# Two-layer mixture kernel: samples issued ahead of two broadcasts, three weight splits moved to GpSimd, and a new order of the last steps

## The chip, the cores and the metric

One core of one Trainium2 chip runs the whole program. The metric is the time of one execution on the device in microseconds (us). TensorE (PE) multiplies matrices, VectorE (DVE), ScalarE (ACT) and GpSimd (POOL) do elementwise work, and each has its own instruction stream. SyncE (SP) issues nearly all DMAs. The engines meet only at semaphores.

## The reference

128 sequences of 64 tokens and 256 features go through two conditional layers, in float32:

```
h = gelu(x @ Wi[e] + bi[e]);  r = h @ Wo[e] + bo[e] + x      # e: one of 8 experts of the sequence
y = normalize(r, 1e-12) * gamma[e] + beta[e]
a = gelu(y @ down_W.T + down_b)                              # 256 -> 64
o = a @ expert_W[d].T + expert_b[d], or a where d is invalid # d: one of 16 domains of the sequence
u = (o + emb[d]) @ up_W.T + up_b + y
out = normalize(u, 1e-5) * ln_gamma + ln_beta
```

## The kernel before, in words

**Tiles.** The sequences are sorted by expert on the chip. A tile is two sequences (128 tokens), and there are 64 tiles. The last four are mixed: their two sequences can have different experts, so most of their instructions exist once per half.

**Precision.** Every float32 operand of a large product is held as a high and a low half in float16, and a product takes three matmuls (high by high, high by low, low by high). For a weight chunk of 128x512, `high` on ScalarE writes the rounded part and `low` on VectorE writes what is left. An expert has 8 chunks: four of Wi and four of Wo.

**Steps.** The function `step(i, ...)` exists once per engine. In step i TensorE runs the first product of tile i (`p_h`, lines 1168 to 1170), the `up` product of tile i-4 (`p_u`, 1207 and 1208), the `down` product of tile i-3 (`p_d`, 1192 to 1194), the second product of tile i-1 (`p_o`, 1179 to 1181) and the transposition of tile i-2 (`p_t`, 1215). Steps 0 to 3 also build the table `ctab` of up_W folded with the experts of layer two, in four rounds (line 1108 on TensorE, 684 on ScalarE, 912 on VectorE). Steps 64 to 68 are the drain: no first product is left, and they run out the tiles in flight.

**What sets the order.** Each engine executes the program as written, and each wait sits in its own place of that order. SP issues in one queue, in program order: at the start the first expert's chunks, the next expert's first four chunks (`stage`), then the broadcast of `bo` and of `gamma` over 128 partitions (1 MB each), then the loads of step 0: `load_turned(2)` (x of tile 2, transposed, line 404) and `load_natural(0)` (line 411). The first product of a tile needs `x_hi` and `x_lo` (lines 698 and 899), which need `x_T`.

**GpSimd.** In step i it adds `bo` to the natural x of tile i-1 (line 630), computes two reciprocal square roots (614 for the first normalization, 635 for the second), multiplies by gamma (609, or 602 and 605 for a mixed tile) and copies the per-expert columns: `gb_tile` (643, for the multiplication of `yT_hi` on ScalarE, line 777) and `bi_tile` (575). Each copy or gamma product of a mixed tile first loads two expert numbers into registers. In step 1 it also runs `split_rows` (lines 554 to 562), which splits the shared rows of the table in three parts. SP sends them out to memory in `added` and back into `ctab`.

Of the kernel before, what the change touches and what calls it, by code (L numbers as in the profile page):

```python
# [4 lines left out]
B, S, D = 128, 64, 256  # L5
# [50 lines left out]
def build(nc, t):  # L56
# [4 lines left out]
    with ctx:  # L61
# [173 lines left out]
        w_first_hi = sem("w_first_hi")  # L235
        w_first = sem("w_first")
# [128 lines left out]

        def late(j):

            return isinstance(j, int) and TILES - 4 <= j < TILES
# [13 lines left out]
        FIRST_ORDER = (0, 2, 1, 3, 4, 5, 6, 7)  # L382

        @block.sync
        def _(sp):
# [61 lines left out]
            def step(i, parity, four, weights):  # L447
# [26 lines left out]
                if exists(i):  # L474
                    load_natural(b[0:2], i, parity)
                if weights and starting:
                    load_chunk()
                if isinstance(i, int) and i == 1:
# [3 lines left out]
                if isinstance(i, int) and i == 2:  # L482
# [3 lines left out]
                    for q in range(PARTS):  # L486
                        sp.dma_start(ctab[A + PARTS + E0 * q:A + PARTS + E0 * (q + 1), :, 1, :],
                                     by_part[q, ENTRIES:ENTRIES + E0, :].unsqueeze(1)
                                     .to_broadcast([E0, ENTRIES, D])).then_inc(added_in, 16)

# [6 lines left out]
        def _(pool):  # L497
# [82 lines left out]
            def step(i, parity, four, weights):  # L580
                e_third, e_before, e_last, _, e_next = indices(pool, i + (IDX_EXP - 3), 5, E0 - 1)
                if exists(i - 5) and not late(i - 5):
# [53 lines left out]
                if exists(i - 2):  # L636

                    need(pool, a1o_done, i - 3)
                    if isinstance(i, int) and i == 2:
                        pool.wait_ge(g_scaled, 1)  # L640
                        pool.wait_ge(downb_ready, 1)
                    for n, e_n in enumerate(experts(i - 2, e_before)):
                        ins = pool.tensor_copy(gb_tile[:, parity, n, :], gb_flat[:, bass.ds(e_n * GB, GB)])
                    ins.then_inc(gb_done, 1)
# [11 lines left out]
        def _(act):  # L656
# [43 lines left out]

            for n, m in enumerate(FIRST_ORDER):

                if n == 2:
                    high_x(0, 0)
                if n == 4:
                    act.wait_ge(beta_down, 1)
                    act.wait_ge(adapter_in, 6 * 16)
                    nc.scalar.activation(gb_c[:, :, KD:KD + 1], ph_flat[1][:, WCH:WCH + E0].unsqueeze(2), ACT.Identity,
# [636 lines left out]
```

## Time and profile before

| | us |
|---|---|
| median of 3 runs | 470.23 (469.9 to 473.76) |
| the profiled execution | 468.74 |
| its span in the profile | 467.0 |
| TensorE busy | 435.8 (93%) |
| VectorE, ScalarE, GpSimd busy | 392.2, 378.4, 343.1 |

The span is what the profile's rows cover, and the profiled execution is 1.74 us longer than it. Times of rows count from the start of the span. A row that says "idle before" gives how long its engine had nothing to run and which operation ended that. The ends of matmul rows are modelled: matmuls overlap, and a row of 0.22 us can stand 0.06 us after the one before it, so the pace is read from the starts.

### The profile page before, as it was taken

The numbers are of one execution on the slowest core, as the hardware profiler recorded it, in microseconds if no ns is written. First come the engines' busy times: TensorE is split into PE (matmuls) and PEld (weight loads), VectorE is DVE, ScalarE is ACT, GpSimd is POOL, SyncE is SP. The second block draws the span as 40 slices with busy tenths as digits, with TensorE's granted clock in tenths as the row PEclk, the third lists the DMA queues.
The fourth block names the chain that finished last, engine by engine and source line by source line (L and its number), as shares of the span: only waits on it lengthen the run. The fifth ranks groups of instructions, "written<-read, shape, count | busy, mean of one in ns | idle before, by whom it ended". The sixth has DMA issues, their size and how long they took to land.

```text
span 467.0 us, 19001 instructions
## 1 busy us (share of the span) xinstructions
PE 435.8 (93%) x5724; PEld 399.7 (86%) x5725; DVE 392.2 (84%) x1049; ACT 378.4 (81%) x1161; POOL 343.1 (73%) x560
## 2 busy tenths in 40 slices
PE   2977999999999999999999999999999999999962
PEld 2765989998999989998999899998999999888951
DVE  7748999998899989998899989998899887776574
ACT  2767988888988888988888988888988877877722
POOL 3035488888788877888788878887788888866652
PEclk9999999999999999999999999999999999999995
DMA  4964234433333333433333333333332222220101
GB/s 105 314 220 94 77 85 132 113 107 108 110 96 97 104 104 107 109 96 98 101 105 104 111 95 96 107 106 107 106 91 78 63 69 63 66 59 27 30 19 34
DMA packets 51178, 45.71 MB, mean 98 GB/s; under 512 B 8820, under 2 KB 42563, under 8 KB 50883
## 3 DMA queue, kind: packets, MB, share of 16 engines
q1 hardware_dynamic: 50385, 45.02, 34.3%
q8 instruction: 20, 0.33, 0.3%
q10 hardware_dynamic: 754, 0.20, 0.2%
q14 instruction: 19, 0.16, 0.1%
HBM read 36.75 MB, written 8.44 MB: 97 GB/s over the span
## 4 chain that ended last, share of the span: by engine, by line
PE 84%; DVE 3%; issue 3%; ACT 3%; SPq 2%; DMA 2%; POOL 2%; POOLq 1%; ACTq 0%; DVEq 0%
PE p_h L1168 12%; PE p_o L1179 12%; PE p_o L1180 12%; PE p_o L1181 12%; PE p_h L1170 11%; PE p_h L1169 11%; PE p_u L1207 3%; PE p_u L1208 3%; PE p_t L1215 3%; DMA x_nat<-in_x 2%; PE p_d L1192 2%; PE p_d L1194 1%; PE p_d L1193 1%; ACT h L729 1%; ACT yT_hi L777 1%
## 5 line engine op out<-in xcount | busy, mean ns | idle before, releaser
L1168 PE MATMUL p_h<-x_hi,W 128*128 128x128 f16 (+1 forms) x1088 | 185.2, 218 | 4.2 <-DVE x_lo L899 2.3
L1170 PE MATMUL p_h<-x_hi,W 128*128 128x128 f16 (+1 forms) x1088 | 184.9, 217 | 0.0
L1169 PE MATMUL p_h<-x_lo,W 128*128 128x128 f16 (+1 forms) x1088 | 184.9, 217 | 0.0
L729 ACT ACTIVATE h<-p_h,bi_tile 128x128 f32<-128x128 f32 (+1 forms) x544 | 149.5, 360 | 0.1
L1179 PE MATMUL p_o<-W,h_hi 128*128 x512 | 139.6, 273 | 0.4 <-DVE r L947 0.4
L1180 PE MATMUL p_o<-W,h_hi 128*128 x512 | 139.6, 273 | 0.0
L1181 PE MATMUL p_o<-W,h_lo 128*128 x512 | 139.6, 273 | 0.0
L1168 PEld LDWEIGHTS p_h<-x_hi,W 128*128 x1088 | 105.8, 98 | 13.2 <-issue 5.5
L1169 PEld LDWEIGHTS p_h<-x_lo,W 128*128 x1088 | 106.1, 99 | 0.8
L1170 PEld LDWEIGHTS p_h<-x_hi,W 128*128 x1088 | 106.0, 98 | 0.0
L933 DVE SCALAR_TENSOR_TENSOR h_lo<-h,h_hi 128x512 f16<-128x512 f32 (+1 forms) x128 | 97.9, 767 | 1.9 <-ACT h_hi L740 1.9
L590 POOL TENSOR_TENSOR y<-y,lng 128x256 f32<-128x256 f32 x60 | 43.7, 728 | 54.6 <-DVE h_lo L933 52.4
L740 ACT ACTIVATE h_hi<-h 128x512 f16<-128x512 f32 (+1 forms) x128 | 80.1, 629 | 2.0
L635 POOL TENSOR_TENSOR rs<-mv,neg_half 128x1 f32<-128x1 f32 x64 | 58.9, 920 | 13.4 <-DVE mv L979 13.1
L754 ACT ACTIVATE a<-p_d,gb_tile 128x128 f32<-128x128 f32 (+1 forms) x68 | 24.1, 360 | 53.8 <-PE p_d L1194 53.8
L630 POOL TENSOR_TENSOR x_nat<-x_nat,bo_t 128x256 f32<-128x256 f32 x60 | 46.6, 776 | 15.3 <-DMA x_nat<-in_x 15.3
L1179 PEld LDWEIGHTS p_o<-W,h_hi 128*128 128x128 f16 x512 | 50.1, 98 | 6.0 <-issue 1.2
L1181 PEld LDWEIGHTS p_o<-W,h_lo 128*128 128x128 f16 x512 | 50.1, 98 | 5.8
L1180 PEld LDWEIGHTS p_o<-W,h_hi 128*128 128x128 f16 x512 | 50.1, 98 | 5.1
L974 DVE SCALAR_TENSOR_TENSOR a1s<-a,a1s 64x128 f16<-64x128 f32 x64 | 22.1, 346 | 34.6 <-ACT a1s L759 34.4
L614 POOL TENSOR_TENSOR rs<-mv,neg_half 128x1 f32<-128x1 f32 x64 | 35.2, 550 | 18.0 <-DVE mv L962 16.1
L777 ACT ACTIVATE yT_hi<-p_t,gb_tile 128x128 f16<-128x128 f32 (+1 forms) x136 | 42.2, 380 | 7.5 <-PE p_t L1215 5.6
(170 smaller groups left out, 935.1 us busy)
## 6 DMA issues: line engine op xcount, KB each, us to landing
stage<-in_w SPq DMA_DIRECT2D x56, 256.0 KB, 2.7
x_nat<-in_x SPq DMA_DIRECT2D x128, 64.0 KB, 2.1
out<-y SPq DMA_DIRECT2D x128, 64.0 KB, 2.0
x_T<-in_xT SPq DMA_DIRECT2D x126, 64.0 KB, 2.0
W<-in_w SPq DMA_DIRECT2D x8, 256.0 KB, 3.8
bo_t<-in_bo SPq DMA_DIRECT2D x1, 1024.0 KB, 7.1
g_t<-in_gamma SPq DMA_DIRECT2D x1, 1024.0 KB, 10.2
W<-in_expert_W SPq DMA_DIRECT2D x2, 128.0 KB, 2.8
```

The lines of the kernel that those rows point to most:

```text
L630: pool.tensor_tensor(x_nat[:, 1 - parity, :], x_nat[:, 1 - parity, :], bo_t[:, bass.ds(e_last * D, D)], ALU.add).then_inc(xb_done, 1)
L635: pool.tensor_tensor(rs[:, 1:2], mv[:, 1, 1:2], neg_half[:, 0:1], ALU.pow).then_inc(rs2_done, 1)
L729: ins = nc.scalar.activation(h[:, c, mine], p_h[parity][:, c, mine], ACT.Gelu, bias=bi_tile[:, parity, n, c:c + 1], scale=1.0 / (XS * WS))
L740: ins = nc.scalar.activation(out, h[:, cols_h, mine], ACT.Copy, scale=HS)
L777: ins = nc.scalar.activation(yT_hi[:, k, mine], turned_z[:, mine], ACT.Copy, scale=gb_tile[:, parity, n, k:k + 1])
L933: ins = v.scalar_tensor_tensor(lo[at], h[:, cols_h, mine], HS, hi[at], ALU.mult, ALU.subtract)
L1168: mm(out, hi, x_high, start=(k == 0), stop=False)
L1169: mm(out, hi, x_low, start=False, stop=False)
L1170: ins = mm(out, lo, x_high, start=False, stop=(k == KD - 1))
L1179: mm(p_o[:, 0:D], h_high[at], hi, start=(j == 0 and n == 0), stop=False)
L1180: mm(p_o[:, 0:D], h_high[at], lo, start=False, stop=False)
L1181: ins = mm(p_o[:, 0:D], h_low[at], hi, start=False, stop=(j == KI - 1 and n == len(places) - 1))
```

## The change

- **SP:** of the next expert's four chunks only the first is issued early. Then come x_T of tile 2 and natural x of tile 0, then `bo`, then the other three chunks, then `gamma`. Step 0 issues neither of the two again. The round trip of `added` moves from steps 1 and 2 to steps 2 and 3, and goes ahead of the chunk load of its step.
- **GpSimd:** the high parts of the first expert's chunks 5, 6 and 7 are made here instead of on ScalarE, and `split_rows` moves from step 1 to step 0.
- **ScalarE and VectorE:** x of tile 1 is split before chunk 4, and the plain entries of `ctab` (lines 717 and 923) move from ahead of step 0 to its end.
- **Drain:** GpSimd copies `gb_tile` at the start of the step. TensorE runs `down` ahead of `up`. ScalarE waits for its own `a1o` before it writes `a1`, and issues the DMA of the second half of the last tile, which SP issued before.

```diff
@@ sync
-            for j in range(AHEAD):
+            load_later(0, expert[0], 0, 0)
+            b = indices(sp, IDX_SP, 4, B - 1)
+            load_turned(b[2:4], 2, 0)
+            load_natural(b[0:2], 0, 0)
+            sp.dma_start(bo_t[:, :], t["bo"].partition_broadcast(P)).then_inc(bo_in, 16)
+            for j in range(1, AHEAD):
                 load_later(j, expert[0], j, j % SLOTS_W)
-            sp.dma_start(bo_t[:, :], t["bo"].partition_broadcast(P)).then_inc(bo_in, 16)
...
-                if exists(i + 2):
+                if exists(i + 2) and not first:
                     load_turned(b[2:4], i + 2, parity)
...
-                    for n in range(2):
+                    for n in range(1 if last_tile(i - 5) else 2):
...
-                if isinstance(i, int) and i == 1:
+                if isinstance(i, int) and i == 2:
 
                     sp.wait_ge(parts_ready, 1)
@@ gpsimd
+                if exists(i - 2) and drain(i):
+                    gather_gb()
                 if exists(i - 5) and not late(i - 5):
...
+                if exists(i - 2) and not drain(i):
+                    gather_gb()
                 if exists(i + 1):
                     gather_bi(e_next, i + 1, 1 - parity)
-                if isinstance(i, int) and i == 1:
+                if isinstance(i, int) and i == 0:
+                    for m in FIRST_ORDER[ACT_FIRST:]:
+                        pool.wait_ge(first_in[m], 16)
+                        pool.tensor_scalar(W[m][:, 0:1, :, 0, :], by_unit(first_stage[m]), WS, None, ALU.mult)\
+                            .then_inc(w_pool_hi, 1)
                     pool.wait_ge(u_ready, 1)
@@ scalar
+                    if drain(i):
+                        act.wait_ge(a1o_done, i - 3)
...
+            b = indices(act, 6 * (STEPS - 1) + IDX_SP + 5, 1, B - 1)
+            act.wait_ge(y_late, TILES - (TILES - 4))
+            act.dma_start(t["out"][bass.ds(b[0] * S, S), :], y[HALF[1], (TILES - 1) % 2, :])\
+               .then_inc(y_out[(TILES - 1) % 2], 16)
@@ vector
+                if n < ACT_FIRST:
+                    dve.wait_ge(w_first_hi, n + 1)
+                else:
+                    dve.wait_ge(w_pool_hi, n + 1 - ACT_FIRST)
@@ tensor
+                    if drain(i):
+                        pe.wait_ge(a1_done, i - 3)
...
+                    if drain(i) and c == UP_AT and exists(i - 3):
+                        down()
                     if c == UP_AT and exists(i - 4):
...
-                    if c == DOWN_AT and exists(i - 3):
+                    if c == DOWN_AT and exists(i - 3) and not drain(i):
                         down()
```

**SP, from the end of the first expert's chunks to step 0.** `x_T` is the transposed x (here of tile 2), `x_nat` the natural x (here of tile 0). Before:

```order
L418 DMA stage<-in_w 128x512
...
L438 DMA bo_t<-in_bo 128x2048
L439 DMA g_t<-in_gamma 128x2048
...
L297 TENSOR_LOAD idx [waits idx_ready]
L404 ISA [waits x_split]
L404 DMA x_T<-in_xT 128x128
...
L411 DMA x_nat<-in_x 64x256
```

The same place in the change:

```order
L428 DMA stage<-in_w 128x512
L298 TENSOR_LOAD idx
L414 ISA [waits x_split]
L414 DMA x_T<-in_xT 128x128
...
L421 DMA x_nat<-in_x 64x256
...
L451 DMA bo_t<-in_bo 128x2048
...
L454 DMA g_t<-in_gamma 128x2048
```

Both sample loads now stand ahead of the two broadcasts, and three of the four chunks stand between the broadcasts.

**GpSimd, step 65 of the drain.** `gb_tile` holds the columns of tile 63, `yg` is the gamma product of tile 62, the first `rs` is the first normalization of tile 63. Before:

```order
L297 TENSOR_LOAD idx [waits yl_done,z1_done]
L602 ISA
L602 TENSOR_TENSOR yg<-z,g_t 64x256
L605 ISA [waits yg_half]
L605 TENSOR_TENSOR yg<-z,g_t 64x256
L614 TENSOR_TENSOR rs<-mv,neg_half 128x1 [waits mv1_done,yg_done]
L635 TENSOR_TENSOR rs<-mv,neg_half 128x1 [waits mv2_done]
L297 TENSOR_LOAD idx [waits a1o_done]
L643 ISA
L643 COPY gb_tile<-gb_c 128x4
```

In the change:

```order
L298 TENSOR_LOAD idx [waits a1o_done]
L605 ISA
L605 COPY gb_tile<-gb_c 128x4
...
L298 TENSOR_LOAD idx [waits yl_done,z1_done]
L630 ISA
L630 TENSOR_TENSOR yg<-z,g_t 64x256
L633 ISA [waits yg_half]
L633 TENSOR_TENSOR yg<-z,g_t 64x256
L642 TENSOR_TENSOR rs<-mv,neg_half 128x1 [waits mv1_done,yg_done]
L663 TENSOR_TENSOR rs<-mv,neg_half 128x1 [waits mv2_done]
```

The wait for `a1o_done` moved from behind the gamma products and both `rs` to the front of them.

**TensorE, step 66 of the drain.** `p_u` is `up` of tile 62, `p_d` is `down` of tile 63. Before:

```order
L1207 MATMUL p_u<-ctab,a1s 128x256 [waits a1o_done,a1_lo,r2_done]
L1208 MATMUL p_u<-ctab,a1o 128x256
...
L1192 MATMUL p_d<-yT_hi,down_hi 128x128 [waits yT_done]
L1193 MATMUL p_d<-yT_lo,down_hi 128x128
L1194 MATMUL p_d<-yT_hi,down_lo 128x128
```

In the change:

```order
L1234 MATMUL p_d<-yT_hi,down_hi 128x128 [waits a1_done,yT_done]
L1235 MATMUL p_d<-yT_lo,down_hi 128x128
L1236 MATMUL p_d<-yT_hi,down_lo 128x128
...
L1300 ISA x2
L1249 MATMUL p_u<-ctab,a1s 128x256 [waits a1o_done,a1_lo,r2_done]
L1250 MATMUL p_u<-ctab,a1o 128x256
```

The two products changed places, in steps 64, 65 and 66.

## Rows read from the trace of the kernel before

**Rows 1.** Busy time by stretch: stretch, its length, then PE, PEld, DVE, ACT, POOL.

```profile
50.00:434.00 384.00, 381.06 (x5144) 354.43 (x5142) 336.57 (x896) 334.02 (x1029) 311.48 (x480) 1.00 0.34 94
```

**Rows 2.** TensorE's waits from 15 to 45 us: in total, times, longest.

```profile
PE p_h L1168 <- DVE x_lo L899: 2.3, 2, 1.3
PE p_t L1215 <- DVE z L986: 1.8, 1, 1.8
PE p_u L1108 <- DVE ctab L912: 1.7, 1, 1.7
PE p_d L1192 <- DVE yT_lo L1016: 1.0, 1, 1.0
```

**Rows 3.** Timeline of ScalarE: start, length, operation, idle before.

```profile
29.99 0.42 ACT L698 ACTIVATE x_hi<-x_T 128x256 f16<-128x256 f32 x1 [4.58 <-DMA x_T<-in_xT]
```

**Rows 4.** Timeline of GpSimd, steps 1 and 2.

```profile
30.56 0.88 POOL L630 TENSOR_TENSOR x_nat<-x_nat,bo_t 128x256 f32<-128x256 f32 x1 [15.34 <-DMA x_nat<-in_x]
...
31.99 0.39 POOL L558 CAST W<-W 128x256 f16<-128x256 f32 x1
...
32.91 1.00 POOL L562 TENSOR_TENSOR W<-W 128x256 f32<-128x256 f32 x1
...
36.22 0.39 POOL L560 COPY W<-W 32x256 f16<-32x256 f16 x1
```

**Rows 5.** DMA issues from 0 to 45 us: count, KB each, median us to landing.

```profile
bo_t<-in_bo SPq DMA_DIRECT2D x1, 1024.0 KB, 7.1
g_t<-in_gamma SPq DMA_DIRECT2D x1, 1024.0 KB, 10.2
```

**Rows 6.** Timeline of SP's queue: start and length of issuing.

```profile
15.76 1.94 SPq L418 DMA_DIRECT2D stage<-in_w  x4
...
17.74 0.42 SPq L438 DMA_DIRECT2D bo_t<-in_bo  x1
...
20.96 0.88 SPq L404 DMA_DIRECT2D x_T<-in_xT  x2
...
41.33 0.34 SPq L485 DMA_DIRECT2D ctab<-added  x1
```

**Rows 7.** The tile ctab from 36 to 60 us: its first reader in `up`.

```profile
L1207 PE MATMUL p_u<-ctab,a1s x4: 269/272/273, 50.3 to 56.8; 128*128 x4
```

**Rows 8.** Timeline of GpSimd in the drain.

```profile
449.47 0.72 POOL L602 TENSOR_TENSOR yg<-z,g_t 64x256 f32<-64x256 f32 x1 [0.26 <-issue]
...
453.33 0.55 POOL L614 TENSOR_TENSOR rs<-mv,neg_half 128x1 f32<-128x1 f32 x1 [2.23 <-DVE mv L962]
...
454.90 0.38 POOL L643 COPY gb_tile<-gb_c 128x4 f32 x2
...
456.68 0.72 POOL L605 TENSOR_TENSOR yg<-z,g_t 64x256 f32<-64x256 f32 x1 [0.19 <-POOL yg L602]
```

**Rows 9.** Timeline of ScalarE in the drain.

```profile
451.14 0.78 ACT L785 ACTIVATE a1o<-a,gb_tile,keeps 128x64 f16<-128x64 f32 x2
...
455.38 0.93 ACT L777 ACTIVATE yT_hi<-p_t,gb_tile 128x64 f16<-128x64 f32 x4 [1.47 <-POOL gb_tile L643]
```

**Rows 10.** Timeline of TensorE in the drain, steps 65 to 67.

```profile
454.58 0.44 PE L1215 MATMUL p_t<-ident,z 128*128 128x128 f32 x2 [1.57 <-DVE z L986]
457.10 0.37 PE L1207 MATMUL p_u<-ctab,a1s 128*128 x1 [2.08 <-ACT a1o L785]
...
457.90 0.31 PE L1192 MATMUL p_d<-yT_hi,down_hi 128*128 128x128 f16 x1
...
460.45 0.37 PE L1207 MATMUL p_u<-ctab,a1s 128*128 x1 [1.70 <-ACT a1o L785]
```

**Rows 11.** Timeline of VectorE in the drain, step 66.

```profile
458.14 0.43 DVE L957 SCALAR_TENSOR_TENSOR yg<-p_u,yg 128x256 f32<-128x256 f32 x1 [0.95 <-PE p_u L1208]
...
459.81 0.29 DVE L974 SCALAR_TENSOR_TENSOR a1s<-a,a1s 64x128 f16<-64x128 f32 x1
```

**Rows 12.** Timeline of SP's queue at the end: the last tile's two halves.

```profile
463.93 1.14 SPq L472 DMA_DIRECT2D out<-y  x2
```

More of the change, by code:

```diff
@@ L235, in build @@
         w_first_hi = sem("w_first_hi")
+        w_pool_hi = sem("w_pool_hi")
         w_first = sem("w_first")
@@ L364, in drain, with last_tile @@
             return isinstance(i, int) and i >= TILES
+        def last_tile(j):
+            return isinstance(j, int) and j == TILES - 1
         def late(j):
@@ L382, in build, with by_unit @@
         FIRST_ORDER = (0, 2, 1, 3, 4, 5, 6, 7)
+        ACT_FIRST = 5
+        def by_unit(staged):
+            return staged.rearrange("p (a u q) -> p a u q", a=1, u=2)
         @block.sync
@@ L463, in step @@
                     b = record[6 * parity:6 * parity + 6]
-                if exists(i + 2):
+                first = isinstance(i, int) and i == 0
+                if exists(i + 2) and not first:
                     load_turned(b[2:4], i + 2, parity)
@@ L489, in step @@
                                      .to_broadcast([E0, ENTRIES, D])).then_inc(added_in, 16)
+                if weights and starting:
+                    load_chunk()
             run(sp, step, NCH, AHEAD, 2 * LEAD)
@@ L581, in step, with gather_gb @@
                 e_third, e_before, e_last, _, e_next = indices(pool, i + (IDX_EXP - 3), 5, E0 - 1)
+                def gather_gb():
+                    need(pool, a1o_done, i - 3)
+                    if isinstance(i, int) and i == 2:
+                        pool.wait_ge(g_scaled, 1)
+                        pool.wait_ge(downb_ready, 1)
+                    for n, e_n in enumerate(experts(i - 2, e_before)):
+                        ins = pool.tensor_copy(gb_tile[:, parity, n, :], gb_flat[:, bass.ds(e_n * GB, GB)])
+                    ins.then_inc(gb_done, 1)
+                if exists(i - 2) and drain(i):
+                    gather_gb()
                 if exists(i - 5) and not late(i - 5):
@@ L699, in high_x @@
                     .then_inc(xhi_done, 1)
[L701 removed]
+            for n, m in enumerate(FIRST_ORDER[:4]):
                 if n == 2:
                     high_x(0, 0)
[L705 to L708, printed above, removed]
[L709 to L711 removed]
                 act.wait_ge(first_in[m], 16)
                 high(m, 0, first_stage[m]).then_inc(w_first_hi, 1)
[L716 to L718 removed]
+            act.wait_ge(beta_down, 1)
+            act.wait_ge(adapter_in, 6 * 16)
+            nc.scalar.activation(gb_c[:, :, KD:KD + 1], ph_flat[1][:, WCH:WCH + E0].unsqueeze(2), ACT.Identity,
+                                 bias=downb[:, :]).then_inc(downb_ready, 1)
+            act.wait_ge(u_summed, 1)
+            nc.scalar.copy(u_s[:, :], ph_flat[1][:, 0:D]).then_inc(u_ready, 1)
+            high_x(1, 1)
+            for m in FIRST_ORDER[4:ACT_FIRST]:
+                act.wait_ge(first_in[m], 16)
+                high(m, 0, first_stage[m]).then_inc(w_first_hi, 1)
             def gelu(i, parity, half):
@@ L743, in step @@
             def step(i, parity, four, weights):
-                if exists(i + 1):
+                if exists(i + 1) and not (isinstance(i, int) and i == 0):
                     high_x(i + 1, 1 - parity)
@@ L791, in step @@
                     high_h(i, parity, 1)
+                if isinstance(i, int) and i == 0:
+                    act.wait_ge(up_in, 2 * 16)
+                    nc.scalar.activation(ctab[:, E1:ENTRIES, 0, :], upT[:, :].unsqueeze(1).to_broadcast([P, 2, D]),
+                                         ACT.Copy, scale=CS).then_inc(c_plain_hi, 1)
                 if isinstance(i, int) and i == 1:
@@ L1057, in step @@
                     normal_1()
-                if exists(i + 1):
+                if exists(i + 1) and not (isinstance(i, int) and i == 0):
                     low_x(i + 1, 1 - parity)
@@ L1072, in step @@
                     low_y()
+                if isinstance(i, int) and i == 0:
+                    dve.wait_ge(c_plain_hi, 1)
+                    v.scalar_tensor_tensor(ctab[HALF[0], E1:ENTRIES, 1, :], rows(upT[HALF[0], :], 2), CS,
+                                           ctab[HALF[0], E1:ENTRIES, 0, :], ALU.mult, ALU.subtract).then_inc(c_plain, 1)
                 if isinstance(i, int) and i == 1:
```

26 lines of the change are left out of this document (4 added, 22 removed).

## The prediction

> **What bounds the kernel now.** I read the busy time by stretch first. From 50 to 434 us TensorE is busy 381.06 of 384.00 us [rows 1]: the middle is its own, the change does not touch it, and what is won or lost at either end passes through unchanged. So I read the waits of TensorE at the start, then the timelines of the engines it waits for, and last the drain from 449 us.
>
> At the start TensorE waits four times where the change acts: 1.3 us for `x_lo` of tile 2, 1.7 for `ctab` of round 1, 1.8 for `z` of tile 0, 1.0 for `yT_lo` of tile 0 [rows 2]. (The other wait in the 2.3 of the first row is before the first matmul.) They have one source. `x_T` of tile 2 is issued at 20.96 [rows 6], behind 2 MB of broadcasts that land at 17.74 + 7.1 = 24.8 (`bo`) and 10.2 after their issue (`gamma`) [rows 5]. ScalarE stands still for 4.58 us until 29.99 [rows 3], and its `ctab` copies, its `h` and its `yT_hi` are late with it. GpSimd stands still for 15.34 us until natural x of tile 0 is there at 30.56. Then it runs `split_rows` from 31.99 to 36.22 + 0.39 = 36.61 [rows 4], ahead of the `rs` that `z` of tile 0 needs.
>
> In the drain the chain runs from one engine to the next and every wait is short, so each place in an engine's order counts.
>
> **The start.** SP issues a chunk in 1.94 / 4 = 0.49 us [rows 6]. Without three chunks ahead of them the sample loads go out near 17.2 (0.9 us of it for their addresses) instead of 20.96, with only the chunks still queued in front. A landing near 21 is my estimate; ScalarE needs it at 29.99 - 4.58 = 25.4, and the 0.5 us for the plain table entries that now stand ahead of that place are taken from an earlier one. So `x_hi` of tile 2 comes 4.6 us earlier. TensorE ends the second product of tile 0 no earlier than before, so of those 4.6 us the first wait gives only its 1.3; the `ctab` copies of round 1 come earlier by the same 4.6, so the 1.7 goes too. On GpSimd `split_rows` (4.6 us) runs from about 21 to 26 beside work that doesn't need it, `bo` lands near 24 (it has 0.75 MB of chunks less and 0.25 MB of samples more in front), so `rs` of tile 0 waits for VectorE alone and the 1.8 goes. The 1.0 on `yT_lo` goes if ScalarE holds its lead. Sum: 1.3 + 1.7 + 1.8 + 1.0 = 5.8 us.
>
> What could be late next: ScalarE and VectorE then run without a break until step 3, and by adding up their operations `yT_lo` of tile 0 comes about 0.4 us before TensorE wants it. Chunk 1 of the next expert now stands behind `bo` and must be there at 25.4 + 0.4 = 25.8. The order of the queue says about 25. And the `ctab` writes from `added` move back one step. Before, they went out at 41.33 [rows 6] and were wanted at 50.3 [rows 7]; after, they wait behind natural x of tile 3, so I put their issue near 38.8 and the want at 44.5, 5.7 us later against 9.0. I take 0.1 us for these three together and 0 to 1 as the range. **Start: 5.7 us won.**
>
> **The three high parts on GpSimd.** No row has this operation. The nearest cheap one is a cast of 128x256 in 0.39 us, so 0.8 for 512 columns; the dear end is the two-input subtraction of 128x256 at 1.00, so 2.0 [rows 4]. I take 1.0, nearer to the cast, since it has one input too. VectorE's low parts of these chunks stand ahead of its round-0 entries of `ctab`, which TensorE wants at about 25.8. From 17.9, when chunk 5 should be there by its issue, three at 1.0 end at 20.9 and VectorE is through at about 25.1. From 1.5 us each TensorE waits, 3 us for every further microsecond: 1.5 us at the dear end. Cost taken: 0. The work that falls away on ScalarE is worth nothing by itself, since it stood still for 4.58 us right after [rows 3].
>
> The Trainium skill, "GPSIMD Engine Reference", sections 1 and 4.1, says that one-input work on GpSimd is roughly at line rate, two-input work about twice as slow, and that it shares its memory interface with VectorE instructions that have two inputs there, which the low parts are. By that the operations of the two engines could follow each other instead of overlapping and the sum would lose some tenths more at the start; no row before has this pair, so the bounds above stand.
>
> **The drain, columns first.** In step 65 GpSimd used to multiply tile 62 by gamma at 449.47, in the shade of TensorE's last long product, and was free when `rs` of tile 63 came due at 453.33 [rows 8]. Now the copy of `gb_tile` stands in front, and it waits for `a1o` of tile 61, which ends at 451.14 + 0.78 = 451.92 [rows 9]. After that: 0.7 for the wake-up and the load of two expert numbers (copy starts at 452.6), then from that copy to the end of the second gamma product as before, 456.68 + 0.72 - 454.90 = 2.5 (until 455.1), then `rs` at 455.2 instead of 453.33: 1.87 later. Before, `rs` ended at 453.88 and the transposes at 454.58 + 0.44 = 455.02 [rows 10], 1.14 later; now 455.75 + 1.14 = 456.9. `yT_hi` of tile 63 waited at 455.38 for its columns [rows 9]. The columns are now early, and it starts at about 456.95: 1.5 later. The same move in step 64 pushes GpSimd by about 1.4, which ends before 450.
>
> **The drain, down first.** In step 66 `up` of tile 62 started at 457.10 and `down` of tile 63 at 457.90 [rows 10]. `down` was ready at about 457.2 by `yT_lo`. With the 1.5 it is ready at 458.8, runs 0.65 at the slow pace (four matmuls of `up` took 0.8 there, half clock, 1.2 GHz), and `up` follows at about 459.4, so VectorE's `yg` of tile 62 starts at 460.3 instead of 458.14. On VectorE the low part of `a1s` of tile 63 stands 459.81 - 458.14 = 1.67 behind it [rows 11], so it ends at 460.3 + 1.67 + 0.29 = 462.3, and the last `up` starts at 462.5 instead of 460.45 [rows 10]: **2.05 lost.** Even with `yT_hi` in time, down first alone would push that `up` by about 0.5, because `a1s` on VectorE hangs behind `yg`. The wait for `a1o` on ScalarE is for its own work of the step before: 0.
>
> **The last half by ScalarE.** SP issues two halves in 1.14 us, 0.57 each plus the address [rows 12]. The second leaves beside the first: **0.65 won**, 0.5 to 0.7.
>
> **Sum.** -5.7 + 2.05 - 0.65 = -4.3 us. Against the profiled execution, 468.74 - 4.3 = 464.4 (span 462.7). That execution is 1.5 us under the median of the runs, and I make the forecast against the median: 470.23 - 4.3 = **465.9 us**. 1% is 4.7 us, about what a measurement of this kernel can tell from no change, so the bound for faster is 465.5.
>
> **The rivals.**
> - *The sum holds*: 465.9, chance 0.45. Its own spread is 0.7 us, so four in ten of it lie under 465.5.
> - *The drain costs nothing*: GpSimd or TensorE is not on the path as I read it, the move hides, and only the 0.65 is left: 470.23 - 5.8 - 0.65 = 463.8. For it speaks that `yT_hi` did wait for its columns for up to 1.47 us [rows 9], which is what the move attacks; against it that the columns were only 0.26 us behind the transposes (455.28 against 455.02). Chance 0.22.
> - *The start gives less*: GpSimd at 2.0 us each (1.5 lost) or the ports, chunk 1 or the table writes late by as much: 467.5. For it speak the slacks of 0.4 us and less; chance 0.24.
> - *Slower*: chunk 1 of the next expert lands with the end of the queue. ScalarE then stops at the chunk as it did at the sample, and each microsecond after 25.8 costs TensorE one. `gamma`, issued right behind `bo` at about 18.2, landed at 18.2 + 10.2 = 28.4 [rows 5, 6], and `x_T` of tile 2, the last thing ScalarE waited for, at 29.99 [rows 3]; the loads behind it ended at about 31. At 31.1 the start keeps 5.7 - 5.3 = 0.4, and the drain's 1.4 outweighs it: 471.2. It turns to slower from a landing at 30.1. Against it: the chunk is issued ahead of `gamma`, and `bo` did land at 24.8, long before `gamma`. Chance 0.06.
> - *It does nothing at the start*, because the sample loads wait for something else: the load for tile 2 also waits for `x_lo` of tile 0. Against it: SP gets there only after the first chunk, issued at 15.76 [rows 6], when that is done. 470.2 + 1.4 = 471.6, chance 0.03.
>
> The Trainium skill, "TensorE: Matmul & The Clock Gate", part 1, says that an idle array falls to half clock. The last steps agree: four matmuls of 256 columns take 457.90 - 457.10 = 0.8 us [rows 10], the pace of 1.2 GHz, after a pause of 2.08. A longer pause before the transposes of step 65 could add 0.2 us of half clock to the drain; the sum does without it.
>
> **Chances and range.** Faster by over 1%: 0.45 x 0.4 + 0.22 = 0.40, and 0.02 of the third case, 0.42. Slower by over 1% (over 474.9): 0.04, for what I have not seen. Within 1%: 0.54. The range takes the second case with its 6.2 + 0.65 (463.3), the third, and the unknown costs' ends: 463.0 to 468.8.
>
> **What would show it.** Right: `x_hi` of tile 2 near 25.2 with no idle on ScalarE, TensorE without the four waits, `rs` of tile 63 about 1.9 later against the end of the last long product, the last `up` 2 later, one output issue per queue at the end. Wrong: high parts on GpSimd over 1.5 us, ScalarE idle before its chunk 1, an idle TensorE before the first `up`, or a last `up` that isn't later.

## The result: 1.7 to 2.3 us faster, where 4.3 were forecast

| | before | changed |
|---|---|---|
| median of 20 runs each | 470.69 (469.16 to 473.76) | 468.98 (466.83 to 471.16) |
| ratio | | 0.9951, 95% interval 0.9935 to 0.9967 |
| profiled execution, its span | 468.74, 467.0 | 469.78, 468.0 |

The change saves 1.7 us by the medians and 0.49%, or 2.3 us, by the ratio; its interval lies wholly under 1. The forecast was 465.9, with a range up to 468.8; the median lies 0.2 above that range. The profiled execution of the changed kernel is 0.8 above its median, that of before 2.0 below, so the two spans must not be subtracted. I cut each execution at three marks instead, the transposes of tile 4, 60 and 62 (starts in us):

| execution | tile 4 | 60 | 62 | end | 4 to 60 | 62 to end |
|---|---|---|---|---|---|---|
| before | 67.98 | 431.40 | 449.92 | 467.0 | 363.4 | 17.1 |
| before, once more | 67.55 | 430.92 | 449.45 | 466.5 | 363.4 | 17.1 |
| changed | 64.63 | 430.52 | 448.96 | 468.0 | 365.9 | 19.1 |
| changed, once more | 64.60 | 429.04 | 447.39 | 466.5 | 364.4 | 19.1 |

The start won 2.9 to 3.4 us (forecast 5.7). Three kernels of the experiments leave the start as it is in the changed kernel (e1, e4 and e11); their marks of tile 4 are 63.96, 63.76 and 65.01, so the start itself varies by 1.25 us between executions, and differences of some tenths at this mark say little. The drain with the output lost 2.0 (forecast 2.05 - 0.65 = 1.4). The stretch between, which no edit touches, differs by up to 2.5 us between executions; the last section shows what goes with it.

**The start in the changed kernel.** TensorE's waits from 15 to 50 us (in total, times, longest) answer to [rows 2]:

```profile
PE p_t L1148 <- DVE ctab L947: 2.7, 1, 2.7
PE p_h L1208 <- DVE x_lo L934: 1.0, 1, 1.0
PE p_d L1234 <- DVE yT_lo L1052: 1.0, 1, 1.0
```

The waits for `x_lo` of tile 2 and for `z` are gone. What is left of `x_lo` is the wait ahead of the first matmul. The wait for `yT_lo` is as long as before, and there is one of 2.7, for the table entries of round 0. It is 1.3 in the second execution. It is not wholly new, though: [rows 2] come from one execution of before, and the other has in place of the 1.3 for `x_lo` of tile 2 a wait of 1.3 for the same entries:

```profile
PE p_t L1108 <- DVE ctab L912: 1.3, 1, 1.3
```

Timeline of ScalarE (start, length, operation, idle before), to be read beside [rows 3]:

```profile
21.28 0.63 ACT L683 ACTIVATE W<-stage 128x512 f16<-128x512 f32 x1 [2.81 <-DMA stage<-in_w]
...
26.51 0.44 ACT L723 ACTIVATE x_hi<-x_T 128x256 f16<-128x256 f32 x1
...
32.78 0.42 ACT L723 ACTIVATE x_hi<-x_T 128x256 f16<-128x256 f32 x1 [0.78 <-DMA x_T<-in_xT]
```

`x_hi` of tile 2 starts at 26.51 without a pause, 3.5 us earlier than the 29.99 of before. The sample of tile 3 is now the late one. The pause of 2.81 is one that the forecast did not have: ScalarE waits for chunk 0 of the next expert, issued at 15.84 and landed at 21.26. GpSimd and VectorE, beside [rows 4]:

```profile
19.00 4.47 POOL L671 TENSOR_SCALAR W<-W 128x512 f16<-128x512 f32 x3 [3.71 <-DMA W<-in_w]
...
27.03 2.14 POOL L578 TENSOR_TENSOR W<-W 128x256 f32<-128x256 f32 x1
```

```profile
18.50 0.69 DVE L938 SCALAR_TENSOR_TENSOR W<-W 128x512 f16<-128x512 f32 x1
20.58 1.10 DVE L938 SCALAR_TENSOR_TENSOR W<-W 128x512 f16<-128x512 f32 x1 [1.39 <-POOL W L671]
22.04 1.09 DVE L938 SCALAR_TENSOR_TENSOR W<-W 128x512 f16<-128x512 f32 x1 [0.36 <-POOL W L671]
23.50 0.86 DVE L938 SCALAR_TENSOR_TENSOR W<-W 128x512 f16<-128x512 f32 x1 [0.36 <-POOL W L671]
...
26.16 0.67 DVE L947 SCALAR_TENSOR_TENSOR ctab<-p_t,ctab 64x512 f16<-64x512 f32 x1
```

A high part on GpSimd takes 4.47 / 3 = 1.49 us, and VectorE waits for each one. The low part beside it takes 1.10 where the one before took 0.69, and a subtraction of `split_rows` takes 2.14 where it took 0.67 to 1.00 before. The first high part starts at 19.00, when its chunk is there (18.40 in the second execution), and not at 17.9 as forecast. So the low part of round 0's entries starts at 26.16, and TensorE goes on at 27.48 (27.35 in the second execution), where in the two executions of before it went on at 25.77 and 26.66.

**The drain in the changed kernel,** GpSimd, TensorE and VectorE, answering to [rows 8, 10, 11]. The transposes of tile 62 are at 448.96 here and were at 449.92, so 0.96 has to be added for a comparison:

```profile
451.86 0.31 POOL L605 COPY gb_tile<-gb_c 128x4 f32 x2 [2.29 <-ACT a1o L809]
...
454.43 0.55 POOL L642 TENSOR_TENSOR rs<-mv,neg_half 128x1 f32<-128x1 f32 x1
```

```profile
455.48 0.69 PE L1257 MATMUL p_t<-ident,z 128*128 128x128 f32 x2 [3.26 <-DVE z L1022]
458.09 0.29 PE L1234 MATMUL p_d<-yT_hi,down_hi 128*128 128x128 f16 x1 [1.92 <-DVE yT_lo L1052]
...
461.86 0.37 PE L1249 MATMUL p_u<-ctab,a1s 128*128 x1 [2.10 <-DVE a1s L1010]
```

```profile
459.80 0.42 DVE L993 SCALAR_TENSOR_TENSOR yg<-p_u,yg 128x256 f32<-128x256 f32 x1 [1.77 <-PE p_u L1250]
...
461.47 0.29 DVE L1010 SCALAR_TENSOR_TENSOR a1s<-a,a1s 64x128 f16<-64x128 f32 x1
```

`rs` of tile 63 comes 454.43 + 0.96 - 453.33 = 2.06 later (forecast 1.87) and the last `up` 461.86 + 0.96 - 460.45 = 2.37 later (forecast 2.05). The output leaves in one issue by ScalarE beside SP's:

```profile
465.35 0.57 ACTq L829 DMA_DIRECT2D out<-y  x1
```

### The profile page after: what moved, and what is told of

The parts are those of the page before. It is cut to its first block, busy times and chain, and to the rows that moved or that the text cites. A ratio compares the mean times of both kernels' runs of the same rounds, so it can differ in the third digit from the quotient of the medians.

```text
span 468.0 us, 19008 instructions
## 1 busy us (share of the span) xinstructions
PE 436.9 (93%) x5724; PEld 397.8 (85%) x5725; DVE 396.1 (85%) x1049; ACT 378.8 (81%) x1158; POOL 359.5 (77%) x563
## 4 chain that ended last, share of the span: by engine, by line
PE 84%; POOL 3%; DVE 3%; ACT 3%; issue 3%; DMA 2%; POOLq 1%; SPq 0%; DVEq 0%; ACTq 0%
PE p_h L1208 12%; PE p_o L1219 12%; PE p_o L1220 12%; PE p_o L1221 12%; PE p_h L1210 11%; PE p_h L1209 11%; PE p_u L1249 4%; PE p_t L1257 3%; PE p_u L1250 3%; PE p_d L1234 2%; PE p_d L1236 2%; PE p_d L1235 1%; ACT h L751 1%; DMA W<-in_w 1%; POOL W L671 1%
## 5 line engine op out<-in xcount | busy, mean ns | idle before, releaser
L969 DVE SCALAR_TENSOR_TENSOR h_lo<-h,h_hi 128x512 f16<-128x512 f32 (+1 forms) x128 | 95.9, 752 | 0.5 <-ACT h_hi L762 0.4
L663 POOL TENSOR_TENSOR rs<-mv,neg_half 128x1 f32<-128x1 f32 x64 | 58.0, 907 | 17.2 <-DVE mv L1015 16.9
L1010 DVE SCALAR_TENSOR_TENSOR a1s<-a,a1s 64x128 f16<-64x128 f32 x64 | 26.4, 413 | 35.3 <-ACT a1s L783 35.0
L591 POOL COPY bi_tile<-bi_c 128x8 f32 x68 | 45.8, 677 | 8.4 <-DVE idx L930 8.0
L620 POOL TENSOR_TENSOR y<-y,lnb 128x256 f32<-128x256 f32 x60 | 43.7, 729 | 4.7
```

Source lines behind the costliest of these rows:

```text
L591: ins = pool.tensor_copy(bi_tile[:, parity, n, :], bi_c[:, bass.ds(e_n * KI, KI)])
L663: pool.tensor_tensor(rs[:, 1:2], mv[:, 1, 1:2], neg_half[:, 0:1], ALU.pow).then_inc(rs2_done, 1)
L969: ins = v.scalar_tensor_tensor(lo[at], h[:, cols_h, mine], HS, hi[at], ALU.mult, ALU.subtract)
```

## The experiments

Theory: the order of SP's queue alone wins at the start. The high parts on GpSimd, and what they do to the operations of VectorE beside them, cost again what the other moves could have given, and the drain's two moves cost by their places in the order. Main rival: the drain cost less than it seemed, and the loss lay in the middle. Below, "under before" is the difference of the medians of runs on the same chip; e5 to e8 ran on one chip and the other experiments on a second, where the changed kernel has no runs. The mark "tile 4" is that of the table above.

### e1_old_drain: the drain of before

The edits of e11 and e4, whose diffs stand under the next heading, in one.

> The changed kernel with the drain of before: columns of gb_tile behind rs again, up ahead of down; the last half still by ScalarE, the start untouched. Theory (the drain moves cost time; from the last transposes of a pure step at 449.12 to the end the changed kernel took 18.9 us against 16.9, and 0.4 of output won is hidden in it): 2.4 us come back, 468.98 - 2.4 = 466.6, rs of tile 63 again about 4.3 us after those transposes and not 5.3. Rival (the drain's chain is set elsewhere and only this one execution showed it long): under 0.7 us, 468.3 or more.

Measured: 464.64 against 469.61, ratio 0.9887 (0.9868 to 0.9905), 5.0 under before. From tile 62 to the end it takes 16.7 us. Its `rs` of tile 63:

```profile
449.86 0.55 POOL L640 TENSOR_TENSOR rs<-mv,neg_half 128x1 f32<-128x1 f32 x1 [2.23 <-DVE mv L994]
```

That is 3.42 after the transposes of tile 62 (446.44), as before (3.41), and not 5.47. The 4.3 that I had written was a slip: it took the changed kernel's mark for both kernels. The drain's moves cost 19.06 - 16.69 = 2.4 us, and the rival falls. The last half by ScalarE is what is left against before: 17.06 - 16.69 = 0.37 us won, and not 0.65.

### e4_up_first and e11_columns_last: the two moves apart

e4 takes back TensorE's order and the two waits that came with it:

```diff
-                    if drain(i):
-                        act.wait_ge(a1o_done, i - 3)
-                    if drain(i):
-                        pe.wait_ge(a1_done, i - 3)
-                    if drain(i) and c == UP_AT and exists(i - 3):
-                        down()
-                    if c == DOWN_AT and exists(i - 3) and not drain(i):
+                    if c == DOWN_AT and exists(i - 3):
```

and e11 only GpSimd's:

```diff
-                if exists(i - 2) and drain(i):
-                    gather_gb()
-                if exists(i - 2) and not drain(i):
+                if exists(i - 2):
```

> The changed kernel with only TensorE's order of the drain back (up ahead of down, with the two waits that came with it gone); the columns of gb_tile stay first on GpSimd. By the working of the forecast 1.4 of the drain's cost comes from GpSimd and 0.65 from the order of TensorE: 468.98 - 0.65 = 468.3, rs of tile 63 as late as in the changed kernel, last up 0.6 earlier. Rival (the order is the whole cost): 466.6, as with the whole drain of before.

> The changed kernel with only GpSimd's order of the drain back (rs ahead of the columns of gb_tile); TensorE keeps down ahead of up. The other half of the drain's two moves: from the transposes of tile 62 to the end it took 19.04 with both, 18.46 with columns first alone, 16.74 with neither. The forecast gave down first alone 0.5 and columns first 1.4 to 1.5 of it: so 17.2 here, and 2.3 minus 0.5 = 1.8 under the changed kernel, 4.1 under before. Rival (down first only costs where z is late already): 16.7.

Measured: e4 466.19 against 469.61, ratio 0.9923 (0.9899 to 0.9948), 3.4 under before. e11 465.80 against 469.44, ratio 0.9913 (0.9896 to 0.9930), 3.6 under. Both gained more than their moves are worth, so the drain is read from the traces (tile 62 to the end):

| neither | down first | columns first | both |
|---|---|---|---|
| 16.69 | 17.41 | 18.47 | 19.06 |

TensorE in e11, the transposes of tile 63, the next `down`, and the last `up`:

```profile
451.66 0.69 PE L1255 MATMUL p_t<-ident,z 128*128 128x128 f32 x2 [1.54 <-DVE z L1020]
454.34 0.29 PE L1232 MATMUL p_d<-yT_hi,down_hi 128*128 128x128 f16 x1 [1.99 <-DVE yT_lo L1050]
...
458.11 0.37 PE L1247 MATMUL p_u<-ctab,a1s 128*128 x1 [2.10 <-DVE a1s L1008]
```

The waits for `down` and for `a1s` are nearly those of the changed kernel (1.92, 2.10), but `z` is not late. Columns first costs 1.8 and down first 0.7, and they nearly add up. The forecast's 1.4 to 1.5 and 0.5 to 0.65 were of the right kind, each 0.1 to 0.4 low. The rival, down first free once `z` is in time, falls.

### e2_highs_scalar and e3_both: the high parts back on ScalarE

```diff
-        ACT_FIRST = 5
+        ACT_FIRST = FIRST_CHUNKS
```

e3 has this and e1's edit.

> The changed kernel with the three high parts back on ScalarE (in the place behind x_hi of tile 2), nothing else. Theory (GpSimd's 1.49 us each and the stretched low parts on VectorE, 1.10 for 0.69, made the new wait of 2.7 us for round 1 of ctab): the low parts of the last of them end about 2 us earlier, near 22.3, the wait shrinks to 0.7 or less, 468.98 - 2.0 = 467.0. Rival (the chunks' landing sets it, the first of the three started only as its chunk came at 19.00): the low parts still end near 24 and the time stays within 0.5 of 469.0. Second rival (ScalarE pays what GpSimd saved: 1.9 us more work ahead of its chunk 1, which waited 2.8 us for its landing): 0, since that pause covers it.

> Both edits in one: high parts on ScalarE and the drain of before, on top of the sample loads sent ahead and the last half by ScalarE. If the two costs add: 468.98 - 2.4 - 2.0 = 464.6. If the start's gain is given back in the steady loop (the changed kernel's profile had lost 2.4 of its 3.4 us there by tile 62): about 466.6, the same as with the drain alone.

Measured: e2 466.16, ratio 0.9924 (0.9906 to 0.9941), 3.5 under before. e3 464.07, ratio 0.9881 (0.9861 to 0.9902), 5.5 under. The marks of tile 4 are 64.2 and 64.5, no better than the 64.6 of the changed kernel and the 64.0 of e1. VectorE was indeed through early, but ScalarE ran into the next late sample. In e3:

```profile
33.05 0.42 ACT L721 ACTIVATE x_hi<-x_T 128x256 f16<-128x256 f32 x1 [2.30 <-DMA x_T<-in_xT]
```

and TensorE's waits in it are:

```profile
PE p_d L1228 <- DVE yT_lo L1048: 2.2, 1, 2.2
PE p_h L1204 <- DVE x_lo L930: 1.2, 1, 1.2
PE p_t L1144 <- DVE ctab L943: 0.4, 1, 0.4
```

So part of my theory fell too: the wait of 2.7 goes, as I said, but the marks do not follow, since x_T of tile 3 comes after all the broadcasts (its second half issued at 25.39, landed at 33.03, 7.6 us). The 467.0 expected of e2 was therefore nearly met (466.16) without its reason. On the same chip e3 is 0.6 us under e1, with intervals that overlap, so what the high parts cost here is not told apart from nothing.

### e5_tile3_scalar and e6_tile3_gpsimd: the sample of tile 3 ahead of gamma

```diff
+            load_turned(indices(sp, IDX_SP + 8, 2, B - 1), 3, 1)
             sp.dma_start(g_t[:, :], t["gamma"].partition_broadcast(P)).then_inc(g_in, 16)
...
-                if exists(i + 2) and not first:
+                if exists(i + 2) and not (isinstance(i, int) and i < 2):
```

e5 is e3 with this, e6 is e1 with this.

> The kernel with high parts on ScalarE and the drain of before, and turned x of tile 3 sent ahead of gamma and the layer-norm rows instead of behind them. Theory (the start is now bounded by that sample: ScalarE stood still for 2.30 us until 33.05 before x_hi of tile 3, and TensorE then 2.2 us for yT_lo): the pause goes, tr of tile 1 starts at 43 or earlier instead of 45.2 and the time falls by 2 us against the kernel without the move (464.1 on the last chip, 5.5 under before), so about 7.5 under before. Rival (VectorE and ScalarE are the bound of steps 1 to 3 by the sum of their work): the pause goes but TensorE's waits stay, under 0.7 us won.

> The same move of tile 3's sample, with the three high parts on GpSimd. There ScalarE's pause before x_hi of tile 3 was 0.68 us only, since the high parts on GpSimd had made everything 0.7 us late; so at most 0.7 us is to be had, about 5.7 under before. If high parts on GpSimd cost nothing once the sample is early (what the forecast said of them), this one ends equal to the one with ScalarE; if they cost (1.49 each, with VectorE's low parts stretched), it ends 1 us or more behind it.

Measured on one chip: e5 464.27 against 469.70, ratio 0.9866 (0.9844 to 0.9888), 5.4 under before, tile 4 at 63.48. e6 465.85, ratio 0.9913 (0.9894 to 0.9933), 3.9 under, tile 4 at 64.30. In e5 `x_hi` of tile 3 starts at 31.64 without a pause, as the theory has it, but only 1.05 us come of it at tile 4 (64.53 in e3), not 2. With the sample early, the high parts on GpSimd cost 1.6 us in the medians; the intervals of e5 and e6 do not overlap. At tile 4 the difference is 0.8, but TensorE's first product started 0.7 earlier in e6 (16.10) than in e5 (16.80). It waits for the sample of tile 0, whose load no edit touches. Counted from that product to tile 4, e5 takes 46.7 us and e6 48.2, again 1.5. In the six executions with the high parts on GpSimd TensorE's wait for the entries of round 0 is 0.8 to 2.7 us; in the nine others it is 0 to 0.8, and once, in before, 1.3. VectorE's four low parts in a row, in e5 (GpSimd runs `split_rows` beside them):

```profile
18.60 3.54 DVE L935 SCALAR_TENSOR_TENSOR W<-W 128x512 f16<-128x512 f32 x4
```

### e7_samples_only: nothing but SP's new order

The kernel before with the changed kernel's SP program. Both output halves stay with SP:

```diff
+            load_later(0, expert[0], 0, 0)
+            b = indices(sp, IDX_SP, 4, B - 1)
+            load_turned(b[2:4], 2, 0)
+            load_natural(b[0:2], 0, 0)
             sp.dma_start(bo_t[:, :], t["bo"].partition_broadcast(P)).then_inc(bo_in, 16)
+            for j in range(1, AHEAD):
+                load_later(j, expert[0], j, j % SLOTS_W)
```

> The kernel before with nothing but the new order of SP's queue (samples ahead of the broadcasts; output halves both by SP). Forecast's view (the four waits had the late sample as their one source): most of the start's 4.1 us comes from this alone, 3 us or more, and the rest of the start's edits add little: 469.6 - 3 = 466.6. Rival (the reordering on ScalarE and GpSimd was needed to use the early sample: with split_rows in step 1 z of tile 0 stays late, and high x of tile 1 stands behind the chunks): 1 us, 468.6.

Measured: 465.65 against 469.70, ratio 0.9904 (0.9884 to 0.9923), 4.1 under before and 2.4 under the changed kernel on the same chip. Tile 4 is at 64.49: **the whole gain of the start, 3.1 to 3.5 us, comes from the queue's order**, and the moves on ScalarE, VectorE and GpSimd add nothing to it. Counted from the first product, e7 takes 47.1 us to tile 4, the five executions with the changed kernel's start 47.2 to 48.1, and before 50.9 and 51.4. There is no wait for `z` of tile 0 either, though `split_rows` stands in step 1: the early natural x alone removes it here, and e9, with `split_rows` in step 1 too, has 0.6 of it. The same four low parts with GpSimd still take 2.50 us:

```profile
18.94 2.50 DVE L909 SCALAR_TENSOR_TENSOR W<-W 128x512 f16<-128x512 f32 x4 [0.17 <-ACT W L664]
```

### e8_after_again and e13_before_again: the controls

Both kernels unchanged, so there is no diff.

> The changed kernel unchanged, once more. Its first profiled execution had lost 2.4 us between tile 4 and tile 60 against that of before, where other kernels with the same loop lost 0.1 to 0.5. If that belongs to the execution: 363.4 to 364.0 us between the transposes of tiles 4 and 60, time 467.3 on a chip where before takes 469.6. If it belongs to the kernel: 365.9 again. The wait for ctab of round 1 (2.7 us then, 0.8 and 1.1 in two kernels with the same start) should fall to about 1, the drain stay 2.0 longer than before's.

> The kernel before unchanged, once more, for the trace. If the start of the one execution of before is typical: transposes of tile 4 at 68.0 again, within 0.5, from tile 62 to the end 17.0. The loop between tile 4 and tile 60 took 363.3 to 365.9 in the executions of the kernels with an unchanged loop; if the first execution of before (363.4, 1.5 us under its median) was a lucky one there, this one takes more, 364 to 366. If the start itself varies by more than 1 us, the gains read from one trace of before are that uncertain.

Measured: e8 468.09 against 469.70, ratio 0.9950 (0.9930 to 0.9969); e13 469.43 against 469.34, ratio 1.0003 (0.9989 to 1.0017). Their marks are in the first table. These two starts repeat within 0.5 us and the drains within 0.1. The 365.9 between tiles 4 and 60 belongs to that one execution. Before's 363.4 came again, but that doesn't show that it is typical: the profiled execution of e13 (468.28) is the fastest of its ten, and the first one of before (468.74) is under the fastest of the 20 runs (469.16). No trace of a slower execution of before exists.

### e9_split_step1 and e10_few_edits: are the engines' moves worth anything once the samples are early?

e9 is e5 with `split_rows` in step 1 again:

```diff
                             .then_inc(w_pool_hi, 1)
+                if isinstance(i, int) and i == 1:
                     pool.wait_ge(u_ready, 1)
```

e10 is e7 with tile 3's sample ahead of gamma (the diff of e5) and the last half by ScalarE:

```diff
-                    for n in range(2):
+                    for n in range(1 if last_tile(i - 5) else 2):
...
+            act.wait_ge(y_late, TILES - (TILES - 4))
+            act.dma_start(t["out"][bass.ds(b[0] * S, S), :], y[HALF[1], (TILES - 1) % 2, :])\
+               .then_inc(y_out[(TILES - 1) % 2], 16)
```

> The kernel with high parts on ScalarE, the drain of before and tile 3's sample ahead of gamma, and now split_rows on GpSimd behind natural x of tile 0 in step 1 again, as before the change. Theory A (split_rows in step 0 stretches VectorE's low parts, 0.88 each for 0.63 in the kernel with only the new queue order, and gains nothing): VectorE is through with the low parts 1 us earlier, near 21.4, but rs of tile 0 again waits for GpSimd (1.0 us in that kernel); the time stays within 0.7 of the kernel without the edit, 6.3 under before. Theory B (the forecast's: split_rows ahead of rs costs 1.8 us, so its move was worth that): 1.8 slower, 4.5 under before.

> The kernel before with three edits of SP's and ScalarE's queues alone: samples of tile 2 ahead of the broadcasts, turned x of tile 3 ahead of gamma, last half of the output by ScalarE. No operation of an engine moves. If the engines' reordering in the change is worth nothing: start 1 us better than with the first edit alone (4.5 under before), and 0.3 at the end: 5.8 under before, equal within 0.7 to the best so far (6.3 under). If that reordering is needed once the samples are early: 4.8 under before.

Measured: e9 464.40 against 469.44, ratio 0.9903 (0.9877 to 0.9928), 5.0 under before, tile 4 at 63.02. e10 464.09, ratio 0.9889 (0.9874 to 0.9904), 5.4 under, tile 4 at 62.76, the earliest of all kernels that leave nothing out. Theory B of e9 asked for 1.8 us slower: the trace has 0.5 faster up to tile 4, the median is 0.4 less far under before, and the ratio's interval just overlaps that of e5. B falls, and a small effect either way stays open. e10 shows that no operation has to change its engine or its place among the engines' operations. The medians of e5 and e10 are equally far under before, and their intervals overlap, so which of the two is best is not told apart. Both beat the changed kernel.

### e12_short_round: whose is the wait for yT_lo?

e10 with this, and a memset of the entries in question by GpSimd near the start of the program:

```diff
+                    d = slice(0, 16 if r == 2 else D)
-                    v.scalar_tensor_tensor(ctab[HALF[0], e, 1, :],
-                                           banks[n][HALF[0], :].rearrange("p (a d) -> p a d", d=D), CS,
-                                           ctab[HALF[0], e, 0, :], ALU.mult, ALU.subtract).then_inc(c_copied, 1)
+                    v.scalar_tensor_tensor(ctab[HALF[0], e, 1, d],
+                                           banks[n][HALF[0], :].rearrange("p (a d) -> p a d", d=D)[:, :, d], CS,
+                                           ctab[HALF[0], e, 0, d], ALU.mult, ALU.subtract).then_inc(c_copied, 1)
```

> The kernel with few edits (samples of tiles 2 and 3 sent ahead, last half by ScalarE), in which VectorE's two low parts of round 2 of ctab cover 16 of 256 columns each; the rest of those low parts is left out (set to zero by GpSimd near the start of the program). Theory (TensorE's 1.0 us for yT_lo of tile 0, there before and in every kernel since, is not the late sample's: it is the 1.2 us that these two operations stand ahead of yT_lo on VectorE, and they also free the bank that down writes): yT_lo ends about 0.9 us earlier, the wait shrinks to 0.2 or less, the transposes of tile 1 come at 42.1 instead of 42.9 and the time is 0.8 lower, about 6.0 under before. Rival (the forecast's: the wait hangs on when ScalarE reached yT_hi): the wait stays at 1.0, since nothing moves on ScalarE.

Measured: 463.54 against 469.34, ratio 0.9869 (0.9837 to 0.9901), 5.8 under before. VectorE in e10, then in e12:

```profile
36.57 0.67 DVE L928 SCALAR_TENSOR_TENSOR ctab<-p_u,ctab 64x512 f16<-64x512 f32 x1
37.17 0.67 DVE L928 SCALAR_TENSOR_TENSOR ctab<-p_d,ctab 64x512 f16<-64x512 f32 x1
37.77 0.59 DVE L1032 SCALAR_TENSOR_TENSOR yT_lo<-p_t,gb_tile,yT_hi 128x128 f16<-128x128 f32 x2
```

```profile
37.17 0.17 DVE L930 SCALAR_TENSOR_TENSOR ctab<-p_u,ctab 64x32 f16<-64x32 f32 x1
37.27 0.17 DVE L930 SCALAR_TENSOR_TENSOR ctab<-p_d,ctab 64x32 f16<-64x32 f32 x1
37.36 0.59 DVE L1034 SCALAR_TENSOR_TENSOR yT_lo<-p_t,gb_tile,yT_hi 128x128 f16<-128x128 f32 x2
```

The wait for `yT_lo`, 1.0 us in e10, no longer shows among TensorE's waits:

```profile
PE p_h L1186 <- DVE x_lo L916: 0.6, 1, 0.6
PE p_u L1225 <- DMA ctab<-added: 0.5, 1, 0.5
PE p_t L1126 <- DVE ctab L930: 0.2, 1, 0.2
```

And the transposes of tile 1 follow those of tile 0 after 7.3 us where it was 8.3 in e10, in both executions of the changed kernel and in both of before. Of this 1.0 us the mark of tile 4 shows only 0.2 against e10, because TensorE's first product started 0.8 later here (16.70 against 15.94); counted from it the gain is 1.0. The medians against before differ by 0.4, with intervals that overlap. The rival falls: this 1.0 us did not hang on ScalarE or on the sample. Only what e2, e3 and e7 have beyond it (1.8, 2.2 and 1.3 in all) goes with a late sample of tile 3. `down` of tile 0 waits for two things here, for `yT_lo` and for the bank that the two shortened operations read; which of them it is was not separated.

## Why the prediction was wrong

**"Start: 5.7 us won" is the step that failed**; 2.9 to 3.4 came. It added up four waits of before as if each had the late sample as its source and nothing else stood behind it. What came instead, 1.0 for `yT_lo` and 1.3 or more for the entries of round 0, is about the 2.5 us by which the start fell short. The four terms one by one:
- `x_lo` of tile 2, 1.3: gone, and by the mechanism given: the sample is no longer behind the broadcasts. e7 shows that this one edit carries the start. In the second execution of before the same 1.3 was spent on round 0's entries.
- `z` of tile 0, 1.8: gone from TensorE's waits. The early sample does all of it in e7 and 1.2 of it in e9, with `split_rows` not moved.
- `ctab` of round 1, 1.7: gone in that place, but a wait for round 0's entries stands ahead of it, 2.7 and 1.3 in the two executions (0 and 1.3 in before). It hangs on VectorE's low parts, which hang on GpSimd's high parts.
- `yT_lo` of tile 0, 1.0: stayed at 1.0. "They have one source" was wrong for this one. Two operations of VectorE stand between, in every one of these kernels (e12). The forecast had `yT_lo` "about 0.4 us before TensorE wants it", by a sum that it doesn't show, though the 1.0 us of before [rows 2] stood against it.

Among what could be late next I looked at chunk 1 and at the `ctab` writes. Chunk 1 was in time (landed at 25.98, wanted at 26.82). The `ctab` writes were not always: TensorE waited 0.4 us for them in the second execution of the changed kernel, 0.6 in e4 and 1.3 in e11, against the 0.1 taken for all these together. What the forecast did not have on its list was x_T of tile 3, which still goes out behind all the broadcasts. It was hidden in the changed kernel (0.78), where GpSimd held everything back, and open in e3 (2.30).

**The high parts on GpSimd, taken at 1.0 us each and a cost of 0.** They took 1.49 each. The range (0.8 to 2.0) held it, and it sits just under the 1.5 from which the forecast let TensorE wait. But they began at 19.00 and not at 17.9, and VectorE's part grew from 0.69 to 1.10. Measured by e5 against e6 the cost is 1.6 us in the medians and 1.5 in the traces from the first product on. In the changed kernel it in part replaced a pause that another late load would have made.

The forecast's sentences by the Trainium skill, "GPSIMD Engine Reference" (section 1: the SBUF interfaces are shared with VectorE, with contention where its instructions have two inputs there), said that the sum "would lose some tenths more". By that rule, the trace agrees in kind: one low part takes 0.69 us alone and 1.10 beside a high part, and four in a row take 2.50 us with GpSimd still and 3.54 beside `split_rows`. The size no row of before could have given.

**The drain, 2.05 lost: 2.4 measured.** The mechanism was right in each step: GpSimd waits for `a1o`, `rs` comes 1.87 later (2.06), the last `up` 2.05 later (2.37). The terms are short by the wake-up (0.90 and not 0.7 from the end of `a1o` to the copy) and by the transposes of step 65, 0.69 at a granted clock of 0.50 against 0.44 at 1.00 [rows 10], which the forecast named and left out.

**The last half by ScalarE, 0.65 won: 0.37 measured.** Taking the issue of 0.57 off the path brought only a part of it.

With the measured terms the sum is -3.2 + 2.4 - 0.4 = -1.2 us, and the medians show -1.7 and -1.6. The range's lower end counts 6.2 for a start that its own case has at 5.8. Of the rivals "the start gives less" (467.5) came nearest, with the right place and too small a size. The cases with a drain that costs nothing and with chunk 1 at the end of the queue did not happen.

What stays open: in most experiments the medians gained more against before than the marks in the traces do, by 0 to 1.2 us (e7: 4.1 against 3.3), and by 1.9 in e2 and e3. The most likely reason, not shown, is that both profiled executions of before are among its fastest. Each kernel has one or two profiled executions, too few to place it.

## What to carry to other kernels

When one late transfer seems to explain several waits, list for each of them what else stands in front of the awaited operation on its own engine; a wait about as long as two neighbouring operations may be theirs, and shortening them tells (e12). When a sample is moved ahead of a broadcast, look at the next one behind it in the queue: here it was late next, and moving it too was the cheapest edit. An operation moved to an idle engine can slow its neighbour (here 0.69 us became 1.10), so before the move is credited as free, both durations have to be priced. And count a start from the first operation that no edit touches: the wait for the first sample alone varied by 1.5 us between these executions.

## What the runs showed of the hardware

**Slipped steps.** Nothing in the change touches the long loop, but it took 363.4 to 365.9 us. ScalarE's waits between 65 and 432 us have a row for it, in the first execution of the changed kernel and in the second:

```profile
ACT yT_hi L801 <- POOL gb_tile L605: 1.4, 8, 0.2
```

```profile
ACT yT_hi L801 <- POOL gb_tile L605: 0.5, 3, 0.2
```

Five steps in a row show what differs, from 330 to 362 us: GpSimd's copy of the columns and VectorE's `a1s`, first in before, then in the changed kernel (busy us, mean ns, idle before):

```profile
L643 POOL COPY gb_tile<-gb_c 128x4 f32 x5 | 1.7, 341 | 0.0
...
L974 DVE SCALAR_TENSOR_TENSOR a1s<-a,a1s 64x128 f16<-64x128 f32 x5 | 1.4, 290 | 2.3 <-ACT a1s L759 2.3
```

```profile
L605 POOL COPY gb_tile<-gb_c 128x4 f32 x5 | 4.7, 942 | 0.0
...
L1010 DVE SCALAR_TENSOR_TENSOR a1s<-a,a1s 64x128 f16<-64x128 f32 x5 | 4.1, 814 | 3.0 <-ACT a1s L783 3.0
```

Both are almost three times as long there, and ScalarE waits for the copy.

Over all 15 executions the stretch from tile 4 to tile 60 grows with the count of those waits: 0 times, 363.3 to 363.5 us; once, 363.6 to 363.8; twice, 363.9 to 364.1; 3 times, 364.4; 4 times, 364.8; 8 times, 365.9. That is some 0.3 us per slipped step, and most of the spread between the traces. What makes a step slip was not tried.

**The clock falls in one idle stretch.** In e3 TensorE stood still for 2.2 us before `down` of tile 0. The stretches around it, with length, busy times and, behind POOL's, the granted clock:

```profile
38.00:40.00 2.00, 0.92 (x17) 0.93 (x18) 1.93 (x6) 1.90 (x5) 0.00 (x0) 1.00 0.05 15
40.00:42.00 2.00, 2.00 (x23) 1.86 (x20) 1.65 (x4) 1.95 (x6) 1.88 (x4) 0.55 0.23 69
42.00:44.00 2.00, 2.00 (x12) 1.31 (x11) 2.00 (x4) 1.20 (x6) 0.83 (x2) 0.60 0.58 112
44.00:48.00 4.00, 4.00 (x46) 3.68 (x45) 3.22 (x8) 3.45 (x9) 0.00 (x0) 1.00 0.37 107
```

After a stretch with 0.92 of 2.00 us busy the clock stood at half (1.2 GHz) for 2 x 2.0 x 0.45 + 2 x 2.0 x 0.40 = 3.4 us, and the transposes of tile 1 came 11.0 us after those of tile 0, where e2 took 9.0. The waits of 0.7 to 1.8 in the same place did not do this in any other kernel, not even in e2, whose TensorE was busy for only 0.60 us of the same stretch and kept 1.00. Why it fell in the one and not in the other stays open. So in e3 a late sample went with two costs, the wait and the half pace after it.
